# Attention with a mixture-of-experts branch: transposes of the probabilities at two steps' distance, value products at six, and a new order in every third step

## The reference, cut to what matters

```
x = L0_attn_x                                   # 16 batches x 512 tokens x 128
xn = (x - mean) / sqrt(var + 1e-5)
# attention, 16 heads of 64
q, k, v = xn @ Wq + bq, xn @ Wk + bk, xn @ Wv + bv
att = softmax(causal(q k^T / 8)) / 8
a = concat_heads(att @ v) @ proj
# experts
base = xn @ W^T
lw = softmax(l2norm(xn @ Wp^T + bp) @ l2norm(sim) * exp(temp))
res = sum over the top expert of lw * (xn @ Wd_i^T) @ Wu_i^T
out = x + a + base + res
```

## Time and profile before

| | us |
|---|---|
| median of 3 runs (1347.4 to 1347.88) | 1347.55 |
| the profiled execution | 1347.42 |
| its span, first to last instruction | 1345.7 |
| PE busy | 1330.3 |
| DVE, ACT, POOL busy | 1106.3, 1085.9, 997.7 |

### The profile page before, as it was taken

The page is one execution under the profiler, slowest core; times in us unless marked ns, Lnnn a source line. Parts: engine busy times, 40 slices in busy tenths (PEclk is TensorE's granted clock), DMA queues, the critical chain, the costliest instruction groups (busy, mean ns, idle before and its releaser), DMA issues.

```text
span 1345.7 us, 34453 instructions
## 1 busy us (share of the span) xinstructions
PE 1330.3 (99%) x10783; PEld 1131.7 (84%) x10783; DVE 1106.3 (82%) x4001; ACT 1085.9 (81%) x3162; POOL 997.7 (74%) x1443
## 2 busy tenths in 40 slices
PE   7999999999999999999999999999999999999998
PEld 5788888888888888888888888888888888888887
DVE  8978888788787878878788787888878888788785
ACT  6887887888788887887888788788888887888785
POOL 7887777778777777777777768777677876778664
PEclk9999999999999999999999999999999999999999
DMA  6455444544544445454444544454454454545541
GB/s 155 95 119 118 103 112 113 122 104 111 125 107 116 105 113 123 103 122 110 116 103 115 123 103 115 112 122 110 103 124 113 103 122 112 122 95 119 118 103 48
DMA packets 112561, 150.59 MB, mean 112 GB/s; under 512 B 18239, under 2 KB 47230, under 8 KB 112382
## 3 DMA queue, kind: packets, MB, share of 16 engines
q1 hardware_dynamic: 111086, 147.97, 46.8%
q10 hardware_dynamic: 1296, 0.42, 0.2%
HBM read 10.69 MB, written 4.19 MB: 11 GB/s over the span
## 4 chain that ended last, share of the span: by engine, by line
PE 95%; ACT 1%; SPq 0%; POOL 0%; DVE 0%; DMA 0%; issue 0%; DVEq 0%; POOLq 0%
PE zp L1323 22%; PE ptp L1297 20%; PE jobp L1167 13%; PE scores L1285 9%; PE scores L1288 7%; PE outp L1335 7%; PE jobp L1172 6%; PE scores L1266 4%; PE scores L1263 3%; PE jobp L1182 1%; PE outp L1344 1%; PE jobp L1187 1%; PE jobp L1360 0%; PE jobp L1177 0%; ACT prob L721 0%; PE outp L1349 0%
## 5 line engine op out<-in xcount | busy, mean ns | idle before, releaser
L632 POOL TENSOR_TENSOR prob<-prob,rden 128x128 f32<-128x128 f32 (+3 forms) x1024 | 712.4, 720 | 247.2 <-DVE rden L971 240.7
L982 DVE CUSTOM_DVE_ANT_0 prob<-scores,mask 128x128 f32<-128x128 f32 (+3 forms) x1024 | 471.7, 488 | 199.8 <-issue 133.3
L721 ACT ACTIVATE prob<-prob,nmax 128x128 f32<-128x128 f32 (+3 forms) x1024 | 567.5, 559 | 12.1 <-DVE nmax L982 5.4
L1297 PE MATMUL ptp<-ident,prob 128*128 128x128 f32 x2560 | 366.9, 274 | 2.1 <-ACT pt L732 1.5
L1297 PEld LDWEIGHTS ptp<-ident,prob 128*128 128x128 f32 x2560 | 295.0, 140 | 27.4 <-POOL prob L632 5.0
L1323 PE MATMUL zp<-pt,v_sb 128*64 128x64 f32 (+3 forms) x4096 | 307.7, 303 | 0.0
L732 ACT ACTIVATE pt<-ptp 128x128 f32<-128x128 f32 (+3 forms) x512 | 221.2, 432 | 102.8 <-PE ptp L1297 102.8
L1323 PEld LDWEIGHTS zp<-pt,v_sb 128*64 128x64 f32 x4096 | 221.6, 137 | 51.2 <-issue 19.7
L994 DVE COPY pt<-ptp 128x128 f32<-128x128 f32 (+3 forms) x512 | 243.3, 475 | 3.9 <-PE ptp L1297 3.1
L571 POOL CAST k_low<-k_lo 64x512 fp32r<-64x512 f32 x256 | 156.0, 609 | 78.0 <-DVE k_lo L866 68.1
L1285 PE MATMUL scores<-k_twice,q_parts 128*128 128x384 f32 (+1 forms) x512 | 200.9, 392 | 0.0
(11 more groups left out here) (192 smaller groups left out, 2003.3 us busy)
## 6 DMA issues: line engine op xcount, KB each, us to landing
k_twice<-k_hi SPq DMA_DIRECT2D x506, 128.0 KB, 2.3
q_parts<-q_lo SPq DMA_DIRECT2D x256, 128.0 KB, 2.4
q_parts<-q_hi SPq DMA_DIRECT2D x254, 128.0 KB, 2.3
xin<-in_L_attn_x_dram SPq DMA_DIRECT2D x16, 256.0 KB, 3.1
xres<-in_L_attn_x_dram SPq DMA_DIRECT2D x16, 256.0 KB, 3.1
out_dram<-osb SPq DMA_DIRECT2D x15, 256.0 KB, 2.6
pt<-in_L_attn_Wq_dram SPq DMA_DIRECT2D x1, 512.0 KB, 4.8
pt<-in_L_attn_Wk_dram SPq DMA_DIRECT2D x1, 512.0 KB, 5.6
```

Of the source, the lines that this page charges most:

```text
L632: nc.gpsimd.tensor_tensor(part, part, scale, ALU.mult).then_inc(pn_ready, 1)
L721: nc.scalar.activation(part, part, ACT.Exp, bias=nmax[:, s % NROT, h:h + 1], scale=-1.0, accum_out=den[:, s % NROT, h:h + 1]).then_inc(p_r ...
L982: nc.vector.tensor_tensor_reduce(out=prob[:, s % NROT, h, 0:cols], in0=scores[bank][:, first_col:first_col + cols], in1=mask[:, S - cols:S ...
L1297: done = nc.tensor.transpose(ptp[h][:, P * j:P * j + P], prob[:, s % NROT, h, P * j:P * j + P], ident[:])
```

## The change

The transposes follow the scores by two steps (before three), the value products by six (before nine), and the evacuations, `z` copies and projections move with them. PE's order in a step becomes score, (in step 1) project, values, transposes, job, (else) project. In step 2 ACT takes the exponentials ahead of its evacuation, and DVE the keys' low half (`subtracted` replaces `evacuated` there) ahead of the reciprocals and its evacuation; so the pad of a key job moves on POOL from behind the normalisation of step 0 to behind that of step 2. One value job moves from step 22 to 5 and is made right behind the scores. Statistics, router and experts' steps are shifted by one to four steps.

```diff
-LAG_T = 3
-LAG_PV = (9, 9)
-LAG_Z, LAG_LOW_Z = 10, 11
-LAG_OUT = ((27, 31, 35, 39), (25, 27, 31, 35))
+LAG_T = 2
+LAG_PV = 6
+LAG_Z, LAG_LOW_Z = 7, 7
+LAG_OUT = ((25, 29, 33, 37), (25, 29, 33, 35))
-V_STEPS = (29, 30, 2, 6, 10, 14, 18, 22)
+V_STEPS = (29, 30, 2, 5, 6, 10, 14, 18)
-STEP_EVAC, STEP_BASE, STEP_OUT, STEP_FINAL, STEP_LORA = 20, 24, 21, 21, 24
-STEPS_STATS, STEP_AGGR, STEP_VAR = (5, 9), 17, 17
-STEP_RSTD, STEP_CENTRE, STEP_SCALE = 18, 19, 21
+STEP_EVAC, STEP_BASE, STEP_OUT, STEP_FINAL, STEP_LORA = 20, 24, 21, 22, 24
+STEPS_STATS, STEP_AGGR, STEP_VAR = (2, 6), 18, 18
+STEP_RSTD, STEP_CENTRE, STEP_SCALE = 19, 20, 22
-STEP_PRODUCTS, STEP_UNORM, STEP_EXPERTS = 3, 4, 7
+STEP_PRODUCTS, STEP_UNORM, STEP_EXPERTS = 3, 7, 9
-STEP_SUMS, STEP_LOGITS, STEP_WEIGHTS, STEP_FIRST, STEP_PARTS = 5, 6, 9, 10, 13
+STEP_SUMS, STEP_LOGITS, STEP_WEIGHTS, STEP_FIRST, STEP_PARTS = 6, 8, 10, 14, 14
+def subtracted(s):
+    if s % NBLK == 2:
+        return [s - 2]
+    return [] if s % NBLK == 3 else [s if s % NBLK == 1 else s - 1]
...
# POOL
                 made = c.fixed(c.job(s))
-                scaled = 0 if setup else c.fixed(c.head(s, 1))
+                scaled = 0 if setup else c.fixed(c.head(s + 2, 1))
...
                     normalise(c, s)
-                    if s in JOBS and JOBS[s][0] == "k" and not (last and s in AHEAD):
-                        pad_low_keys(c, s)
+                    if s % NBLK == 2 and not (last and s - 2 in AHEAD):
+                        pad_low_keys(c, s - 2)
...
# ACT
+                if s == V_STEPS[3]:
+                    job(c, s)
                 unit = due(s, LAG_T, 1, first, tail)
-                if unit is not None:
+                products = s % NBLK == 2
+                if unit is not None and not products:
                     evacuate_pt(c, unit)
...
                 if not tail:
                     exponentials(c, s)
+                if unit is not None and products:
+                    evacuate_pt(c, unit)
...
# DVE
+            def jobs(c, s, last):
+                for js in subtracted(s):
+                    if js in JOBS and not (last and js in AHEAD):
+                        job(c, js)
...
                 maximum(c, s, 1)
+                products = s % NBLK == 2
+                if products:
+                    jobs(c, s, last)
                 router_early(c, s)
                 if not between:
                     follow()
...
-                for js in evacuated(s):
-                    if js in JOBS and not (last and js in AHEAD):
-                        job(c, js)
+                if not products:
+                    jobs(c, s, last)
...
# PE
                 if not tail:
                     score(c, s, first)
...
+                if not tail and s == V_STEPS[3]:
+                    job(c, s)
+                if s % NBLK == 1:
+                    quarters(c, s, first, tail)
+                p = due(s, LAG_PV, NBLK, first, tail)
+                if p is not None:
+                    for h in range(2):
+                        values(c, p, h)
                 unit = due(s, LAG_T, 1, first, tail)
...
                 if unit is not None:
                     transpose(c, unit)
-                if not tail and s in JOBS and not (last and s in AHEAD):
+                if not tail and s in JOBS and s != V_STEPS[3] and not (last and s in AHEAD):
                     job(c, s)
                 if s == STEP_OUT and not first:
                     transpose_sum(c, tail)
-                for h in range(2):
-                    p = due(s, LAG_PV[h], NBLK, first, tail)
-                    if p is not None:
-                        values(c, p, h)
-                for o in range(NOCT):
...
+                if s % NBLK != 1:
+                    quarters(c, s, first, tail)
```

More of the change, by code:

```diff
@@ L98 @@
 STEP_ROUTER, STEP_GATED = 1, 17
-STEP_EVAC, STEP_BASE, STEP_OUT, STEP_FINAL, STEP_LORA = 20, 24, 21, 21, 24
-STEPS_STATS, STEP_AGGR, STEP_VAR = (5, 9), 17, 17
-STEP_RSTD, STEP_CENTRE, STEP_SCALE = 18, 19, 21
+STEP_EVAC, STEP_BASE, STEP_OUT, STEP_FINAL, STEP_LORA = 20, 24, 21, 22, 24
+STEPS_STATS, STEP_AGGR, STEP_VAR = (2, 6), 18, 18
+STEP_RSTD, STEP_CENTRE, STEP_SCALE = 19, 20, 22
 STEP_XRES = 28
-STEP_PRODUCTS, STEP_UNORM, STEP_EXPERTS = 3, 4, 7
+STEP_PRODUCTS, STEP_UNORM, STEP_EXPERTS = 3, 7, 9
 R_CHAIN = 14
-STEP_SPLIT, STEP_SUMMED, STEP_UP, STEP_BIAS_BANK, STEP_BIAS = (10, 14), 17, 18, 20, 22
-FIRST_STATS = (9, 17)
-STEP_SUMS, STEP_LOGITS, STEP_WEIGHTS, STEP_FIRST, STEP_PARTS = 5, 6, 9, 10, 13
+STEP_SPLIT, STEP_SUMMED, STEP_UP, STEP_BIAS_BANK, STEP_BIAS = (10, 14), 17, 19, 20, 22
+FIRST_STATS = (10, 18)
+STEP_SUMS, STEP_LOGITS, STEP_WEIGHTS, STEP_FIRST, STEP_PARTS = 6, 8, 10, 14, 14
 def bank_of(s):
@@ L788, in step @@
                     exponentials(c, s)
+                if unit is not None and products:
+                    evacuate_pt(c, unit)
+                if not tail and s != V_STEPS[3]:
                     if s in evacuated(s) and s in JOBS and not (last and s in AHEAD):
@@ L809, in evacuate_half @@
                 nc.scalar.activation(y_t[:, cols], outp[:, cols], ACT.Copy).then_inc(y_copied, 1)
-            evacuate_pt(c, -3)
-            evacuate_z(c, -2)
             evacuate_pt(c, -2)
@@ L1139, in _ @@
             reciprocals(c, -1)
-            evacuate_pt(c, -3)
             evacuate_pt(c, -2)
-            low_z(c, -2)
             evacuate_pt(c, -1)
@@ L1361, in transpose_sum, with quarters @@
                 done.then_inc(y_ready, 1)
+            def quarters(c, s, first, tail):
+                for o in range(NOCT):
+                    for quarter in range(4):
+                        n = due(s, OCT_STEPS * o + LAG_OUT[o][quarter], UNITS, first, tail)
+                        if n is not None:
+                            project(c, NOCT * n + o, quarter)
             def step(c, s, first=False, last=False, tail=False):
@@ L1426, in project_last @@
                 done.then_inc(o_ready, 1)
-            transpose(c, -3)
+            transpose(c, -2)
             project(c, -2, 2)
-            for h in range(2):
-                values(c, -2, h)
-            transpose(c, -2)
             transpose(c, -1)
```

## The result

The changed kernel takes 1821.3 us (median of 4 runs, 1817.32 to 1829.28), against 1347.72 before: 1.352 times as long (95% interval 1.3482 to 1.3559). The forecast was 1708 us, its range 1655 to 1775. The direction and the main wait were right; the time lies 113 us above the forecast and outside the range.

What follows compares the result with a forecast made beforehand. PE was taken to bound the kernel. 1347.4 - 6 (exit) + 333 (pad) + 22 (512-key unit) + 21 (DVE) - 11 (quarter hidden in the wait) + 2 (tail) = 1708 us; range 1655 to 1775.

Steps and rivals of the forecast that it cites:

- the pad's place: Each pair's first score, except the first pair's, waits 2.62 us on PE for the later pad: 333 us.
- a chain: From step 3's first score through POOL's normalisation and casts to the next pair's first score: 4.70 us.
- step 3's own work: PE's work in step 3, without a quarter of `project` and with two more transposes: 2.08 us.
- the 0.08 for the weight load: At the end of the pad's chain, a weight load not hidden behind a wait adds 0.08 us.
- that the clock would stay at full: PE's clock stays at 1.00 despite the pad waits, as PE is full for 10 of 12.7 us.
- rival A: PE's clock falls to 1.2 GHz behind each pad wait, doubling step 0: 200 us more, 1910 us; chance 0.06.
- the surplus at changes of work: Step 2 on PE: entering value products costs 0.09 us, leaving into transposes 0.06; the step takes 4.1 us.
- DVE's moved work: DVE's work in steps 10, 14 and 25 overruns and delays what follows: 1.3 us a batch, 21 us.
- the small terms: Transposes of the 512-key unit wait 0.1 us, 0.8 in step 21, 22 us in all; keys' transfers stay hidden.
- The exit term: Leaving value products into transposes rather than scores costs PE less: 0.05 us a pair, 6 us saved.
- Rival B: The pad does not hold the scores; PE waits for the 384- and 512-key units' transposes: about 1505 us; chance 0.05.

Runs made afterwards that it cites:

- e1: The changed kernel, with POOL making the pad behind the normalisation of step 1's unit in place of step 2's: 1543.2 us.
- e3: The kernel before, with only the pad moved behind the normalisation of step 2's unit on POOL: 1781.3 us.
- e10: The kernel before with the pad behind step 2's normalisation, plus two 512-column matmuls of constants ahead of each pair's first score: 1676.0 us.
- e8: The kernel before with the pad behind step 2's normalisation, plus eight 512-column matmuls of constants ahead of each pair's first score: 1644.1 us.
- e2: The changed kernel, with ten 512-column matmuls of constants ahead of each pair's first score, their results overwritten: 1755.24 us.
- e11: The kernel before, with step 1's value products ahead of its transposes and, in that step, the change's step 2 order on ACT and DVE: 1372.9 us.
- e5: The changed kernel, pad behind step 1's normalisation, and DVE taking the 384-key unit's reciprocals in step 2: 1518.0 us.

## Why the prediction was wrong

**Right: PE bounds it, and the pad's place is the large term.** 127 waits, a chain of 4.66 us for the 4.70 forecast, step 3's own work 2.04 (step 7 of e1) for 2.08. The chain was read from the trace of before part by part. Its parts on DVE and POOL kept their lengths to 0.01. At its end, PE started 0.10 behind POOL and not 0.05, and the 0.08 for the weight load isn't in the chain: it lies behind the first score (804.44 to 804.64), in step 0.

**Wrong: that the clock would stay at full.** This is the step that failed: the sum took every PE duration at 2.4 GHz, and rival A had a chance of 0.06. Without the 73 us of the clock the time would be some 1748 us, inside the range. The reason I gave against it, that the same instructions keep PE full around the wait, does not hold: the same wait of 2.46 us is followed by full clock in one pair and by 1.2 GHz in another. A's mechanism is what happened, though not in every pair. A's price for one fall, 1.6 us, came out near: it is 1.5 in the changed kernel, 1.6 in e3 and 1.5 in e10 (32 us between e8 and e10, 21 falls). That is partly luck, since A doubled a whole step 0 and nothing else. In fact the steps 0 with a lower clock take 2.87 us on average for 1.75 (step 24 left out), and the rest lies in step 1. How often it falls was wrong in both cases that I had: 48 times, where the forecast had none and A all 127, so 73 us where A had 200. Rows 9 show one idle of 1.57 us at full clock and none longer. They said nothing of 2.6 us, so they gave no ground for 0.06, and the range had to reach towards A's 1910.

The section of the Trainium skill that I cited for A (TensorE: Matmul & The Clock Gate, "HAM oscillation — how this bites in real kernels") was right in kind. But it says that every burst starts slow in its example, whose waits are some 3 to 5 us long. Here PE idled for 2.46 us, and 48 of 127 steps behind the wait ran slow, so I took more from it for A's 1910 us than it says.

**Mis-sized: the surplus at changes of work, and DVE's moved work.** The 47 us between the forecast and e2, read in the profile of e2, are these. The filler's own cost, 11. Step 2 takes 4.18 us and not 4.1: scores behind eight transposes start with 0.09 of surplus, which the prediction had at nothing. The timeline of PE after shows 0.26 from the first to the second, for 0.17:

```profile
822.14 1.03 PE L1313 MATMUL ptp<-ident,prob 128*128 128x128 f32 x8
822.93 0.42 PE L1301 MATMUL scores<-k_twice,q_parts 128*128 128x384 f32 x1
823.19 0.34 PE L1304 MATMUL scores<-k_low,q_parts 128*128 128x384 f32 x1
```

Step 0 takes 1.74 and not 1.67, by the weight load that the sum had in the chain. That is 0.15 a pair, less 0.04 by which the chain is shorter, 14 us. Step 10 has a wait that the prediction missed; these are its rows of DVE and PE in the timeline of e2:

```profile
910.41 0.76 DVE L1052 TENSOR_TENSOR lg<-lg,row 128x16 f32<-128x16 f32 x1
911.09 0.74 DVE L881 SCALAR_TENSOR_TENSOR q_lo<-jobp,bqk,q_hi 128x512 fp32r<-128x512 f32 x1
911.76 0.41 DVE L993 CUSTOM_DVE_ANT_0 prob<-scores,mask 128x256 f32<-128x256 f32 x1
...
912.57 0.44 PE L1305 MATMUL scores<-k_twice,q_parts 128*128 128x384 f32 x1 [0.37 <-DVE nmax L993]
```

The router's logits, now in step 8, hold up `q_lo` and step 9's maxima, and the second head's score of step 10 waits for their bank: 0.64 us once a batch, 10 us. Then there is a term that the sum didn't have at all. The change moves the statistics of the next inputs from steps 5 and 9 to 2 and 6, and DVE can reach them before the inputs have landed. This is DVE in the changed kernel, in the step 2 with the longest such wait:

```profile
1369.65 0.29 DVE L1005 COPY pt<-ptp 128x128 f32<-128x128 f32 x1 [1.18 <-PE ptp L1313]
1372.47 0.49 DVE L841 BATCH_NORM_STATS2 stats<-xin 128x6 f32<-128x128 f32 x2 [2.52 <-DMA xin<-in_L_attn_x_dram]
1372.87 0.67 DVE L993 CUSTOM_DVE_ANT_0 prob<-scores,mask 128x512 f32<-128x512 f32 x1
```

The first maximum of step 3, and with it the chain of the pad, stands behind this wait, which adds up to 14.0 us in the changed kernel, to 10.8 in e2, and stands nowhere in the waits of the kernel before. The step 3 behind it takes 4.96 us on average in e2 for 4.66, 5 us in 16 batches. The last 7 us I did not assign. The term for DVE's overruns in steps 10, 14 and 25 was right in size: steps 11, 15, 23 and 27 take 0.14, 0.21, 0.33 and 0.65 more than 4.66, 1.33 a batch for the 1.3 of the sum.

**Right: the small terms.** The 512-key unit waits 0.8 us in step 21 (2.60 us in e2, of which 1.78 is work) and little elsewhere. The keys' transfers release no wait of PE.

**The exit term** was right: 0.04 us a pair for 0.05, shown in e11. **Rival B** would have been 1505 us; e1, where the pad does not hold the scores, is at 1543.

Open: why the clock falls behind one wait and not behind the next of the same length, and more often in e3 than in the changed kernel, where PE idles longer; and which waits make up e5's 170 us. No experiment here separates either.

## What to carry to other kernels

When a step is moved on one engine, look for the first instruction on another engine that counts it, and add the chain between them from the rows of before; here the sum held to 0.04 us. Then ask what the time of a new idle on PE does to the clock: if no row of before has an idle that long at full clock, the lower clock belongs in the range. Price one fall, as rival A did, and let the number of falls run from none to one for each wait. And of an order that shortens distances in a full pipeline, expect the wait to move to the next consumer when the first one is removed, as it did from the pad to the transposes of one unit and on to those of the next.

## What was not expected of the hardware

The clock charges unevenly for equal waits. With the pad wait of the change (PE idle 2.46 us in the pairs shown) it fell behind 48 of 127, and the mean granted clock was 0.950. With 1.27 us more of casts in the wait it fell behind all 127 (0.825). In e3, where PE idles only 1.94 us in the pair shown, it fell behind 86 (0.915), and with a filler of 0.5 us in that wait behind 21, all of them with 2.2 us and more of idle (0.978). Each fall cost 1.5 to 1.6 us in the changed kernel, e3 and e10. Work of no use in a wait can therefore be a gain: ten discarded matmuls in each of 127 waits made the changed kernel 66 us faster, and twenty transposes did the same.
